# Four of a set's seven block products summed in one PSUM bank, with ScalarE copying the running sum between them

## The reference, cut to what matters

```
q = y @ Wq    k = y @ Wk    v = y @ Wv
p = softmax(q @ k.T * 192**-0.5, causal, inside each sequence of 32)
x = x + (p @ v) @ Wo
```

## Time and profile before

| | us |
|---|---|
| median of 3 runs | 2130.61 (2130.25 to 2132.34) |
| the profiled execution, first to last instruction | 2129.5 |
| TensorE busy | 2099.1 (99%) |
| VectorE busy | 1385.7 (65%) |
| GpSimd busy | 1255.0 (59%) |
| ScalarE busy | 718.2 (34%) |

### The profile page before, as it was taken

The page is one execution under the profiler, slowest core; times in us unless marked ns, Lnnn a source line. Parts: engine busy times, 40 slices in busy tenths (PEclk is TensorE's granted clock), DMA queues, the critical chain, the costliest instruction groups (busy, mean ns, idle before and its releaser), DMA issues. The chain is left out here.

```text
span 2129.5 us, 36889 instructions
## 1 busy us (share of the span) xinstructions
PE 2099.1 (99%) x11922; PEld 1818.7 (85%) x11922; DVE 1385.7 (65%) x2619; ACT 718.2 (34%) x1444; POOL 1255.0 (59%) x1315
## 2 busy tenths in 40 slices
PE   7999999999999999999999999999999999999999
PEld 5888888989898898989888898989887778888887
DVE  8767777676777767665656566565656766655444
ACT  5333232332323232332323233232323644443332
POOL 3578585777767676776758576776746642114220
PEclk9999999999999999999999999999999999999999
DMA  7421112211111226211111211111112200001110
GB/s 241 153 60 48 53 48 82 54 52 47 49 52 44 76 59 220 55 41 41 40 39 42 66 49 39 39 39 39 40 62 78 89 20 0 0 1 40 39 39 20
DMA packets 122615, 122.28 MB, mean 57 GB/s; under 512 B 35249, under 2 KB 101457, under 8 KB 120497
## 3 DMA queue, kind: packets, MB, share of 16 engines
q1 hardware_dynamic: 91697, 109.87, 16.5%
q10 hardware_dynamic: 29568, 7.34, 1.7%
q0 software_dynamic: 1280, 4.20, 0.7%
HBM read 108.13 MB, written 13.28 MB: 57 GB/s over the span
## 5 line engine op out<-in xcount | busy, mean ns | idle before, releaser
L215 PE MATMUL psum<-yc,wh 128*128 128x512 f32 x904 | 360.8, 399 | 0.3 <-PEq L264 0.3
L216 PE MATMUL psum<-yc,wh 128*128 128x512 f32 x904 | 352.5, 390 | 0.0
L217 PE MATMUL psum<-yc,wh 128*128 128x512 f32 x904 | 352.3, 390 | 0.0
L1463 DVE TENSOR_TENSOR resid<-psum,resid 128x512 f32<-128x512 f32 x248 | 171.1, 691 | 138.0 <-PE psum L217 133.7
L215 PE MATMUL psum<-kept,yc 128*128 128x256 f32 x896 | 256.4, 286 | 1.7 <-DVE u L1413 1.0
L217 PE MATMUL psum<-kept,yc 128*128 128x256 f32 x896 | 253.4, 283 | 0.0
L216 PE MATMUL psum<-kept,yc 128*128 128x256 f32 x896 | 253.4, 283 | 0.0
L1016 POOL TENSOR_TENSOR wh<-wh_f,wh 128x256 fp32r<-128x256 f32 x256 | 189.6, 751 | 107.1 <-ACT wh L982 105.1
L1016 POOL TENSOR_TENSOR wh<-raw,wh 128x256 fp32r<-128x256 f32 x192 | 142.6, 743 | 99.1 <-ACT wh L982 99.1
L217 PEld LDWEIGHTS psum<-yc,wh 128*128 128x128 f32 x904 | 169.7, 188 | 36.1
L215 PEld LDWEIGHTS psum<-yc,wh 128*128 128x128 f32 x904 | 170.3, 188 | 31.8 <-issue 0.7
(11 more groups left out here) (367 smaller groups left out, 4925.9 us busy)
## 6 DMA issues: line engine op xcount, KB each, us to landing
raw<-in_attn_w SPq DMA_DIRECT2D x96, 512.0 KB, 4.9
wo_f<-in_attn_w SPq DMA_DIRECT2D x31, 512.0 KB, 4.0
hankel<-kernel_rows SPq DMA_DIRECT2D x32, 256.0 KB, 5.1
y_parts<-stage ACTq DMA_DIRECT2D x56, 128.0 KB, 2.3
yc<-y_parts SPq DMA_DIRECT2D x7, 1024.0 KB, 5.2
resid<-in_xT SPq DMA_DIRECT2D x4, 1024.0 KB, 9.7
outT<-wide SPq DMA_DIRECT2D x16, 256.0 KB, 2.6
kept_f<-in_l_w SPq DMA_DIRECT2D x3, 1024.0 KB, 5.7
```

Source lines behind the costliest of these rows:

```text
L215: pe.matmul(out, w[0], x[0], start=start, stop=False)
L216: pe.matmul(out, w[0], x[1], start=False, stop=False)
L217: return pe.matmul(out, w[1], x[0], start=False, stop=stop)
L1463: dve.tensor_tensor(part, psum[:, 5 + (GH + m) % 3, :], part, ALU.add).then_inc(tail_free, 1)
```

## The change

Per set, four of the products (P1, P6, P5, P3) go to one bank without clearing it in between, so that the bank holds P1, then U2, then U2 + P5, then C12. ScalarE copies the bank after each: P1 to a buffer, U2 to C21's place, U2 + P5 to C22's place, C12 to its own. P7 and P4 are summed in bank 2 in the same way. VectorE makes three adds: C11 = P2 + P1, C22 = (U2 + P5) + P7, C21 = U2 + (P7 + P4). GpSimd makes none. TensorE's order becomes P6, P2, P5, P7, P1 of the next set, P3, P4. P5 waits for the copy of U2, and P3 for the copy of U2 + P5. The number of matmuls, their shapes and operands stay as they are.

```diff
 PROD = {"P1": 0, "P6": 1, "P5": 2, "P2": 3, "P7": 4, "P4": 5, "P3": 6}
-PROD_AT = (1, 4, 5, 6, 7, 9, 10)
+PROD_AT = (1, 4, 6, 5, 7, 10, 9)
 def product_bank(s, j):
-    return (s * 7 + (-3, 0, 1, 2, 3, 5, 6)[j]) % 3
+    chain = s % 2
+    return {3: 1 - chain, 4: 2, 5: 2}.get(j, chain)
...
# GpSimd
-            def mix(it, s):
-                pool.tensor_tensor(destination(s, 1, 1), u3[:], p5, ALU.add).then_inc(c22_done, 1)
-                pool.tensor_tensor(u2[:], u2[:], p5, ALU.add).then_inc(c22_done, 1)
...
# ScalarE
+            def copy_chain(it, s, k, first=False):
+                g = it * SETS + s
+                j = (1, 2, 6)[k]
+                act.wait_ge(prod_done, product_count(g, j))
+                if k == 0 and s in (0, 1, 5) and not (first and s == 0):
+                    act.wait_ge(scores_done, it * 4 + {0: 1, 1: 2, 5: 4}[s])
+                act.activation(destination(s, (1, 1, 0)[k], (0, 1, 1)[k]), psum[:, bank_of(s, j, first), :],
+                               ACT.Copy).then_inc(chain_copied, 1)
...
                 hw.high(act, it, "H1", (0,))
                 store(0)
-                keep_p5(it, 0, first)
+                copy_chain(it, 0, 0, first)
+                hw.high(act, it, "H1", (1,))
+                copy_chain(it, 0, 1, first)
                 if not first:
                     exps(it * 4)
-                hw.high(act, it, "H1", (1, 2, 3))
+                hw.high(act, it, "H1", (2, 3))
                 keep_p1(it, 1)
-                hw.high(act, it, "H1", (4, 5, 6))
+                hw.high(act, it, "H1", (4,))
+                copy_chain(it, 0, 2, first)
+                hw.high(act, it, "H1", (5, 6))
...
                 store(4)
-                keep_p5(it, 3)
+                copy_chain(it, 3, 0)
                 out_high(it * 2 + 1)
+                copy_chain(it, 3, 1)
                 store(3)
                 keep_p1(it, 4)
+                copy_chain(it, 3, 2)
                 hw.high(act, it, "H3", (0,))
-                keep_p5(it, 4)
+                copy_chain(it, 4, 0)
+                hw.high(act, it, "H3", (1,))
                 o_high(it * 4 + 2)
+                copy_chain(it, 4, 1)
                 store(1)
-                hw.high(act, it, "H3", (1, 2, 3))
+                hw.high(act, it, "H3", (2, 3))
...
# VectorE
             def mix(it, s, k):
-                j = (1, 3, 4, 5, 6)[k]
+                j = (3, 4, 5)[k]
...
# TensorE, set 4
                 product(it, 4, "P6")
+                product(it, 4, "P2")
+                prob_times_v(T + 2, 0, 0, sm + 3, it * SETS + 3)
                 product(it, 4, "P5")
-                prob_times_v(T + 2, 0, 0, sm + 3, it * SETS + 3)
-                product(it, 4, "P2")
                 product(it, 4, "P7")
                 output(T + 2, 0, it * 2 + 1)
                 product(it, 5, "P1")
                 output(T + 2, 1, it * 2 + 1)
+                product(it, 4, "P3")
+                output(T + 2, 2, it * 2 + 1)
                 product(it, 4, "P4")
-                output(T + 2, 2, it * 2 + 1)
-                product(it, 4, "P3")
                 output(T + 2, 3, it * 2 + 1)
```

More of the change, by code:

```diff
@@ L211, in const, with mm3 @@
             return consts[:, a:b]
[L213 to L217, removed]
+        def mm3(pe, out, w, x, start, stop, onto=False):
+            pe.matmul(out, w[0], x[0], start=start, stop=False, skip_group_check=onto)
+            pe.matmul(out, w[0], x[1], start=False, stop=False, skip_group_check=onto)
+            return pe.matmul(out, w[1], x[0], start=False, stop=stop, skip_group_check=onto)
         later = {
@@ L1123, in half, with bank_of @@
             return slice(i * SUBS, (i + 1) * SUBS)
+        def bank_of(s, j, first=False):
+            return FIRST_BANK if first and s == 0 and j in (0, 1, 2, 6) else product_bank(s, j)
         def destination(s, g_half, tile):
@@ L1479, in body @@
                     soft_divide(sm)
+                    soft_turn(sm, 1, it * 8)
                 mix(it, 0, 2)
[L1481 to L1484, removed]
                 mix(it, 1, 0)
@@ L1491, in body @@
                 soft_divide(sm + 1)
+                if not first:
+                    for m in range(3):
+                        add_out(T, m, before, 0)
                 mix(it, 1, 2)
                 if not first:
[L1494 to L1499, removed]
-                if not first:
                     add_out(T, 3, before, 0)
-                mix(it, 2, 0)
                 if first:
@@ L1512, in body @@
                     add_out(T + 1, 0, before, 1)
-                mix(it, 2, 2)
+                mix(it, 2, 1)
                 soft_divide(sm + 2)
                 if not first:
-                    add_out(T + 1, 1, before, 1)
-                    add_out(T + 1, 2, before, 1)
-                mix(it, 2, 3)
-                if not first:
-                    add_out(T + 1, 3, before, 1)
-                mix(it, 2, 4)
+                    for m in range(1, KC):
+                        add_out(T + 1, m, before, 1)
+                mix(it, 2, 2)
                 part(4)
+                soft_turn(sm + 2, 1, it * 8 + 4)
                 mix(it, 3, 0)
-                soft_turn(sm + 2, 1, it * 8 + 4)
+                part(3)
                 mix(it, 3, 1)
-                part(3)
                 mix(it, 3, 2)
-                mix(it, 3, 3)
-                mix(it, 3, 4)
+                part(1)
                 mix(it, 4, 0)
-                part(1)
                 o_low(T + 2)
                 mix(it, 4, 1)
-                mix(it, 4, 2)
                 if turned:
@@ L1668, in product @@
                 j = PROD[name]
-                bank = FIRST_BANK if start else product_bank(s, j)
+                bank = bank_of(s, j, start or (isinstance(it, int) and it == 0))
                 g = it * SETS + s
@@ L1768, in body @@
                 product(it, 2, "P6")
+                product(it, 2, "P2")
+                scores(sm + 2, it * SETS + 1)
                 product(it, 2, "P5")
-                scores(sm + 2, it * SETS + 1)
-                product(it, 2, "P2")
                 if not first:
```

185 lines of the change are left out of this document (90 added, 95 removed).

## The result

The changed kernel takes 2207.31 us (2203.17 to 2207.75, four runs) beside 2130.43 for the kernel before: a ratio of 1.0356 estimated from all runs (the two medians give 1.0361), 95% interval 1.0344 to 1.0368. It is slower, as forecast, and 3 us under the forecast of 2210.

What follows compares the result with a forecast made beforehand. TensorE's instruction stream, 99% busy, was taken as the bound. Terms 51 + 8 + 3 + 5 + 1 + 1 - 1.5 gave 67.5, with the clock 81; 2130.6 + 81 = 2212, rounded to 2210 us, range 2188 to 2238.

Steps and rivals of the forecast that it cites:

- Step 1: Set 4: attention output waits for o_high behind a weight cast that hangs on P5; 3.2 us, 16 times, 51 us.
- Step 2: Set 0: P3 waits for the copy of U2 + P5 behind H1's slot 1 cast; 0.5 us, 16 times, 8 us.
- Step 3: Second head pair's scores wait for VectorE's C21 add, queued behind divide and transposes; 0.2 us, 15 times, 3 us.
- Step 4: Set 3, pair 0: P5 waits for the copy of U2 behind part 4's store; 0.6 us, 8 times, 5 us.
- Step 5: Other copies and adds stay covered; P6 at the start waits 1 us, P4 at the end 1 us.
- Step 6: TensorE's clock may fall behind the long waits, 1.7 us each, 0 to 27 us in all; half taken, 14 us.
- not slower: Rival: TensorE never meets the waits, since GpSimd has H3's sums ready in time; 2129 to 2131 us; 3%.
- the short waits alone: Rival: attention output not late, only the waits of steps 2 to 5 stand; 2147 us; 4%.
- More waits: Rival: U2's copy 0.3 us later, sets 0 and 3 and others miss their windows; 2226 to 2242 us; 15%.

Runs made afterwards that it cites:

- e1: The changed kernel with the attention output's high part (o_high) ahead of H3's slot 1 cast on ScalarE in set 4: 2147.95 us.
- e2: The changed kernel with P5 ahead of the values' product in TensorE's order of set 4: 2166.46 us.
- e3: The changed kernel with GpSimd's first sum of H0 to H3 in a buffer of its own, so it waits for P6 and not P5: 2140.21 us.
- e10: The kernel of e1 with VectorE's mix of block (0,2) ahead of the weights' transposes in set 0: 2141.81 us.
- e7: The kernel of e1 with three more ScalarE exchanges, copies ahead of stores or a cast in set 3 and the first iteration: 2141.79 us.
- e6: The kernel of e3 with the same three ScalarE exchanges as e7: 2133.81 us.
- e9: The kernel of e6 with the last iteration's C2 casts ahead of block (5,2)'s copy, and VectorE's mix of block (3,1) ahead of the row's part: 2130.26 us.
- e8: The changed kernel with ten unused 512-column matmuls filling each of the 16 waits of set 4: 2195.98 us.
- e5: The changed kernel with the casts of H3's slots 2 and 3 also ahead of o_high in set 4: 2227.28 us.

## Why the prediction was right, step by step

By the list of gaps between matmul starts beyond the usual distance, in the profiled spans (2129.5 and 2201.3, a difference of 71.8):

| step | forecast | measured |
|---|---|---|
| 1, output behind the cast | 16 x 3.2 = 51 | 16 x (2.82 + 0.10) = 46.7 |
| 2, set 0's P3 | 16 x 0.5 = 8 | 15 x about 0.2 = 3 |
| 3, scores | 15 x 0.2 = 3 | 15 x 0.27 = 4.1, and 1.2 at an output |
| 4, set 3 behind the store | 8 x 0.6 = 5 | 7 x 0.16 to 0.59 = 2.9 |
| 5, first iteration and start | 1 - 1.5 | 6.9 of waits in place of 3.6: +3.3 |
| 5, end | 1 | 2.8 in place of 1.0: +1.8 |
| 6, clock | 14 | 7 falls x 1.46 = 10.2 |
| sum | 81 | 73, of 75.0 in this stretch |

The sum is for the stretch from attention's start to its end, and there the same matmul comes 75.0 us later than in the kernel before, so some 2 us are in no row of the table. Outside this stretch the profiled execution of the changed kernel is 3.2 us faster, 2.1 of it before attention, where it lacks the fall of the clock of the earlier trace rows; that leaves 71.8. The twelve profiled executions come to one and the same matmul just ahead of attention between 86.4 and 88.5 us, so this part is scatter and no gain of the change.

**Step 1** was right in its mechanism, its place and its count: e1, e2 and e3 each take away one link (the place in the list, P5's late place, the overwritten slot) and the wait shrinks by that link. Its size was 0.3 us too large. The forecast had the cast 1.99 us behind the product's end, from the earlier trace rows; it comes 1.67 behind (348.51 - 346.84), because the second sum takes 0.73 us where the earlier trace rows show 0.94, and GpSimd starts 0.09 us after the product where it took 0.15. The forecast named 0.73 as its lower end.

**Step 2** was over-sized for the same reason. One chain of set 0 in the changed kernel, where P3 had its place at 289.03 (0.227 behind the start of the matmul before it, 288.80):

```profile
286.55 0.74 POOL L997 TENSOR_TENSOR wh_f<-raw 128x256 f32<-128x256 f32 x1 [3.27 <-PE psum L217]
...
287.37 0.74 POOL L1000 TENSOR_TENSOR wh_f<-wh_f,raw 128x256 f32<-128x256 f32 x1
...
288.15 0.42 ACT L984 ACTIVATE wh<-wh_f 128x256 fp32r<-128x256 f32 x1 [3.78 <-POOL wh_f L1000]
...
288.47 0.58 ACT L1250 ACTIVATE qk<-psum 128x512 f32<-128x512 f32 x1
...
289.10 0.50 PE L215 MATMUL psum<-yc,wh 128*128 128x512 f32 x1
```

The copy ends at 289.05, 0.02 after P3's place: what was to be 0.5 us is a start 0.07 late and a first matmul 0.1 longer. A forecast of 0.5 us from a chain of five durations can't tell a wait from none; an error of 0.3 in the cast's start, which step 1 hardly feels, takes away most of this term.

**Step 3** held: the add stands right behind the transposes, and e10 proves the place by moving it. What it missed is the second, smaller lateness at the output 10 us on.

**Step 4** held in its kind, at 0.43 us for most. In one instance the store goes out at 332.23 for 0.55, the copy runs from 332.89 to 333.49, and TensorE, whose place was 333.11, resumes at 333.54.

**Step 5** failed for the first iteration. P6's wait for the first copy is there (0.95 us), and before's wait at the second scores is gone. But two copies stand behind a step that is late only in that iteration, and the steps for set 0 and set 1 were called covered by rows of later iterations: the copy of U2 of set 0 behind the first store (1.43 us) and the last copy of set 1 behind V's cast (2.80 us). A third, at set 3's values, is 1.48 there. The exchanges of e7 and e6 took all three out; in their place stand two waits of 0.5 and 0.9 us for copies of set 2, which the 2.80 us had covered. At the end the wait grew by 1.8 for another reason than forecast, the slowed subtraction, as e9 shows.

**Step 6.** The matmuls behind one of the waits in the changed kernel:

```profile
247.80 0.39 PE L217 MATMUL psum<-yc,wh 128*128 128x512 f32 x1
250.85 0.79 PE L215 MATMUL psum<-o_hi,wo 128*128 128x512 f32 x1 [2.66 <-DVE o_lo L1465]
251.43 0.63 PE L216 MATMUL psum<-o_lo,wo 128*128 128x512 f32 x1
251.86 0.63 PE L217 MATMUL psum<-o_hi,wo 128*128 128x512 f32 x1
```

And a stretch behind another of them (length, then PE, PEld, DVE, ACT and POOL busy, the granted clock, DMA):

```profile
151.40:154.40 3.00, 3.00 (x9) 2.32 (x8) 0.69 (x1) 0.00 (x0) 1.03 (x2) 0.50 0.00 0
```

The matmuls start 0.427 us apart and not 0.227: the clock is at 1.2 instead of 2.4 GHz. This follows 7 of the 16 waits of 2.8 us; the forecast had half of 16. From the matmul that waited to the first of another output, the same one in every iteration, it is 54.78 us without a fall and 56.24 with one in pair 0 (means), 54.90 and 56.37 in pair 1: 1.46 more, where the forecast had 1.7. The three other executions took 3.8 to 4.6 us more than the profiled one, at mean clocks of 0.991 to 0.993 against 0.994. Three more falls would make that, which only their mean clocks support. So the falls cost 10 us in the profiled execution and perhaps 14 in the median one; e8 has 11.3 by another way. The rule of the Trainium skill (TensorE: Matmul & The Clock Gate, Part 1) is that the clock falls after idleness and returns after a busy stretch. The traces agree: in attention every fall stands behind a wait, and with the waits filled (e8) there is none.

The total came out right to 3 us with some help from luck: steps 1, 2 and 4 were 11 us too high together, step 3, the first iteration and the end 7 too low. The clock's term was luck too: half of 16 falls was a choice between nothing and all, and a fall is not settled by the wait's length (last section). Of the rivals, "not slower" and "the short waits alone" needed `o_high` to be ready in spite of its place, which the 16 waits exclude; the latter's 2147 is what e1 measured (2147.95), once that place was changed, though its terms were off one by one as in the table. "More waits" did not occur: in the sets that step 5 called covered, the gaps beyond the first iteration are at most 0.3 us.

## What to carry to other kernels

Where one engine is 99% busy, ask of every exchanged line in a helper's list what the moved instruction waits for, and follow that back to its first cause. If it leads to an instruction of the busy engine itself that has come later, the wait is paid in full each time, and taking hundreds of us of work off the helpers doesn't pay a single one of it. First and last iterations need a look of their own: their steps came late for reasons of which the repeated iterations show nothing.

## What the runs showed of the hardware

- Waits of 2.8 us (start to start beyond the usual distance) cost more than their length: the clock fell behind 7 of 16 of them, at 1.46 us each. Behind e2's 16 waits of 1.0 it did not fall once. Behind e5's 16 of 3.4 it fell 10 times, in four of them for about 5 us (2.6 to 2.8 us lost in each of the three that can be compared: 57.43 to 57.65 us against 54.8 to 54.9).
- Whether a wait of 2.8 us is followed by a fall is not settled by its length or place. Two more waits of this length stand in the first iteration (seven traces, 2.64 to 2.83 us) and at the end (nine traces, 2.76 to 2.80 us). Behind these the clock fell 7 times in 16, each time in some executions and not in others.
- A VectorE subtraction of two SBUF operands took 2.03 us in place of 0.29 beside a GpSimd operation of 2.39 us, and much the same in nine traces.
- ScalarE read a PSUM bank between two matmul groups that add to it, three times in a set, with no cost to TensorE that shows beyond the wait for the copy's end (0.58 to 0.60 us each, and 0.05 until TensorE started) and 0.10 for the longer first matmul behind a wait.
